# The opening of an adaLN attention and feed-forward block: all input tiles turned before the projections

## The chip, the cores and the metric

The kernel runs on one core of one Trainium2 chip. The metric is the device time of one execution in microseconds. The kernel before was run three times: 855.94, 863.45 and 854.26 us, median 855.94 us. The profile is of one more execution, which took 855.57 us.

## The reference, cut to what matters

```
mod = (silu(c) @ wmod).reshape(1, 6, 1, 512)          # c: (1,512)   wmod: (512, 3072)
sa, ca, ga, sb, cb, gb = mod                           # shift, scale, gate of attention; the same of the FFN
h  = layernorm(x) * (1 + ca) + sa                      # x: (1024, 512)
q  = rmsnorm(h @ wq_a.T) @ wq_b.T                      # latent of 128, then 32 heads of 64 + 64
ckv, k_pe = split(h @ wkv_a.T)                         # latent of 32 and a shared rotary key of 64
k, v = rmsnorm(ckv) @ wkv_b.T                          # 32 heads
attention, causal, rotary on the pe parts, softmax;  x = x + ga * (attention @ wo.T)
h  = layernorm(x) * (1 + cb) + sb
x  = x + gb * ((silu(h @ gate_w.T * gs) * (h @ up_w.T * us)) @ down_w.T * ds)
```

All is kept at the precision of float32: most products are made as three products of a high part and a rest (`xH`, `xL`: the value rounded to the matmul's own format, and what is left of it).

## The kernel before, in words

**The opening** works for eight tiles of 128 rows of x (`st` 0 to 7). For each tile VectorE takes mean and variance, ScalarE the root; `normalise` subtracts and scales; TensorE turns the tile by four transposes (`turn_inputs`, L501); ScalarE applies scale and shift of the modulation while it empties the bank, in four pieces (`modulate`, L766); VectorE makes the high part (`h_high`, L996), GpSimd the rest (`hL`, L1334); TensorE projects the tile on 288 rows of weights with 3 x 4 matmuls (`project_inputs`, L513) and turns the resulting latents (`turn_latents`, L522, L523) after ScalarE and VectorE have normalised them (`roots`, `scale`). `latents_high` and `latents_low` split them into `QNH`, `QNL`, `KH`, `KL`. These steps are written as one pipeline: in turn `st`, tile `st` is turned, tile `st-1` projected, tile `st-3`'s latents turned. h, its high part and its rest have two buffers each.

Before the pipeline TensorE computes the shift and scale columns of the modulation (`mod_columns(0)` and `(1)`, L482): for each of six modulation vectors the weights are 1 MB in `wmod`; as columns they take 16 float32 matmuls, which the trace shows as 32 instructions that load 128x128 weights and move one column. The columns 2 and 3 (scale and shift of the second layer norm) and the two gates as rows (`mod_rows`, L490, 8 instructions with 512 columns for a gate) are computed later in the opening, between other work. The six vectors pass through three buffers in `PR`.

**Groups of heads.** 32 heads are 8 groups (g) of 4. For each group: folded weights (`w`, L535), projection of the queries in two halves of 512 rows (`even`, `odd`, `lat`, L544), the rotary products on VectorE (`even`, `odd`, L1056 to L1064), the sums (`RE`; for group 0 on VectorE, L1069 and L1070, for later ones on GpSimd, L1354 and L1355), high part on ScalarE (L811), rest (`split_low`, GpSimd L1361; group 0 on VectorE, L1088). The SP queue then sends the queries of a half by four DMAs, one for each head, from `TQ` to `Q` (L402). Then 38 `part`s: products of queries and keys (L554, with a causal mask L558) into one of three side banks, whose row maxima VectorE takes (L1096: 27 into NMa, 11 into NMb). `join` (L1102) and `rows` (L564, L1109) make a row of negative maxima, which SP sends to `Q` (L407). Each side item takes the next of three PSUM banks in a fixed order, and TensorE waits for the bank's `free` semaphore before it writes.

**Windows.** Window w (0 to 7) computes scores (L610 to L612), exponentials, values (L625) and sums of group w; between its 36 units a table places side items: the 38 maxima of group w+1, the query work of group w+2, the row sums. `window_table` gives each item a place (a share of the window) and a busy time of VectorE. The first two groups' side items stand in the opening: group 0's queries (`QUERY_PLACES`), then `PROLOGUE`, which holds group 0's maxima, group 1's query work and the two gates as rows. All engines issue in the order written; window 0 begins when SP's row of maxima has landed (`S_.nd`). After the windows come the output projection and the feed-forward part, which the change does not touch.

## Time and profile before

| | |
|---|---|
| three runs | 855.94, 863.45, 854.26 us (median 855.94) |
| profiled execution | 855.57 us; its span, first to last instruction, 853.8 us |
| TensorE matmul busy | 793.7 us, 93% of the span |
| VectorE busy | 551.0 us, 65% |
| ScalarE busy | 272.2 us, 32% |
| GpSimd busy | 146.5 us, 17% |
| DMA | 60.46 MB, mean 71 GB/s |
| opening, to the first score | 135.57 us |
| mean granted TensorE clock | 0.960 |

The opening is everything up to the first score (L610). Matmuls are pipelined and the profile models their ends, so the busy share of TensorE is not its work at its best pace: the start of one instruction against the start of the next tells its pace. A granted clock of 1.00 is 2.4 GHz, one of 0.50 is 1.2 GHz. Start times are counted from the span's start.

### The profile page before, as it was taken

What the parts mean: (1) busy time and instruction counts of PE and PEld (TensorE: products, weight loads), DVE (VectorE), ACT (ScalarE), POOL (GpSimd) and SP (SyncE); (2) the same over time, 40 slices, a digit from 0 to 9 for tenths busy, and PEclk for the clock granted to TensorE, in tenths of its full rate; (3) what the DMA queues carried; (4) which work ended last, traced back from release to release, by engine and by line L of the source; (5) the groups of instructions that cost most, each with busy time, mean ns of one, the idle gap of its engine ahead of it and who ended that gap; (6) DMA issues with size and microseconds to landing.
All of it is one profiled execution on the core that took longest, in us unless ns stands there. A gap on an engine that the chain in (4) does not pass through costs nothing.

```text
span 853.8 us, 10443 instructions
## 1 busy us (share of the span) xinstructions
PE 793.7 (93%) x3968; PEld 530.2 (62%) x3968; DVE 551.0 (65%) x836; ACT 272.2 (32%) x402; POOL 146.5 (17%) x113
## 2 busy tenths in 40 slices
PE   5678897999999999999999999999898899999997
PEld 5667544555555555555555555544587788886886
DVE  3355694896896997988978978867565333222342
ACT  2361003333333333343333333343344232222120
POOL 1320031221221321411302401010134000000111
PEclk9886697999999999999999999999899899999999
DMA  8300724023213303321330335046000032220000
GB/s 345 116 0 1 211 52 111 20 56 89 51 25 89 75 21 69 74 52 38 74 85 5 74 83 214 2 159 212 1 1 0 10 102 74 74 65 1 25 37 38
DMA packets 35904, 60.46 MB, mean 71 GB/s; under 512 B 4144, under 2 KB 16176, under 8 KB 34064
## 3 DMA queue, kind: packets, MB, share of 16 engines
q1 hardware_dynamic: 34656, 57.11, 23.7%
q10 hardware_dynamic: 1200, 2.69, 0.9%
q8 instruction: 33, 0.54, 0.3%
q14 instruction: 15, 0.12, 0.1%
HBM read 32.40 MB, written 2.10 MB: 40 GB/s over the span
## 4 chain that ended last, share of the span: by engine, by line
PE 64%; DVE 20%; issue 9%; POOL 2%; ACT 2%; DMA 2%; SPq 1%; POOLq 0%; DVEq 0%; ACTq 0%
PE PS L710 14%; PE PS L610 6%; PE PS L554 6%; PE PS L625 6%; DVE PR L1184 6%; PE PS L680 5%; PE PS L611 5%; PE PS L612 5%; DVE NMa L1096 4%; DVE NMb L1096 3%; PE PS L544 2%; PE PS L482 2%; PE PS L570 2%; PE PS L513 2%; PE PS L614 2%
## 5 line engine op out<-in xcount | busy, mean ns | idle before, releaser
L836 ACT ACTIVATE PR<-PS 128x1024 f32<-128x1024 f32 (+1 forms) x144 | 133.0, 929 | 255.2 <-PE PS L612 240.4
L1096 DVE TENSOR_REDUCE NMa<-PS 128x1 f32<-128x512 f32 (+3 forms) x216 | 138.7, 662 | 50.0 <-PE PS L558 42.7
L554 PE MATMUL PS<-KH,Q 96*128 96x512 f32 (+3 forms) x384 | 135.5, 414 | 3.9 <-DVE TQ L1081 1.4
L610 PE MATMUL PS<-Q,KH 97*128 97x512 f32 x288 | 131.7, 457 | 2.6 <-DMA Q<-NM 2.6
L710 PE MATMUL PS<-Q 128*128 128x512 f32 (+1 forms) x528 | 123.2, 396 | 5.1 <-DVE Q L1258 4.5
L710 PEld LDWEIGHTS PS<-Q 128*128 128x128 f32 (+1 forms) x528 | 99.2, 188 | 28.2 <-DVE Q L1258 4.7
L1184 DVE TENSOR_TENSOR PR<-PR 128x2048 f32<-128x2048 f32 (+3 forms) x56 | 109.3, 1951 | 10.2 <-ACT PR L836 8.9
L611 PE MATMUL PS<-Q,KL 96*128 96x512 f32 x288 | 114.7, 398 | 0.0
L612 PE MATMUL PS<-Q,KH 96*128 96x512 f32 x288 | 113.9, 396 | 0.0
L554 PEld LDWEIGHTS PS<-KH,Q 96*128 96x128 f32 x384 | 69.8, 197 | 62.3 <-issue 38.0
L610 PEld LDWEIGHTS PS<-Q,KH 97*128 97x128 f32 x288 | 56.0, 195 | 35.3 <-issue 17.1
L625 PE MATMUL PS<-PR,V 128*32 128x512 f32 (+3 forms) x704 | 73.1, 488 | 0.3 <-ACT PR L836 0.3
L612 PEld LDWEIGHTS PS<-Q,KH 96*128 96x128 f32 x288 | 55.1, 191 | 12.9
L611 PEld LDWEIGHTS PS<-Q,KL 96*128 96x128 f32 x288 | 55.4, 192 | 6.6
L1096 DVE TENSOR_REDUCE NMb<-PS 128x1 f32<-128x384 f32 (+3 forms) x88 | 55.3, 629 | 1.0 <-PE PS L558 0.8
L1271 DVE SCALAR_TENSOR_TENSOR wide<-PS,ffn_s,TQ 128x1024 f32<-128x1024 f32 x10 | 12.8, 1285 | 65.9 <-PE PS L710 65.9
L558 PE MATMUL PS<-maskb,identb 128*128 128x128 bf16 (+2 forms) x176 | 46.0, 261 | 0.0
L1367 POOL TENSOR_TENSOR wide<-wide,RD 128x512 f32<-128x512 f32 x16 | 22.7, 1416 | 130.6 <-DVE RD L1123 130.6
L727 PE MATMUL PS<-DH,Q 128*128 128x512 f32 (+1 forms) x176 | 42.8, 391 | 1.4 <-DVE TQ L1271 1.4
L1354 POOL TENSOR_TENSOR RE<-RT 128x512 f32<-128x512 f32 x14 | 18.0, 1286 | 129.3 <-DVE RT L1064 119.4
L1361 POOL TENSOR_TENSOR TQ<-RE,TQ 128x1024 fp32r<-128x1024 f32 x14 | 33.6, 2403 | 36.3 <-ACT TQ L811 36.3
L1412 POOL TENSOR_TENSOR OT<-TQ,Y 128x512 f32<-128x512 f32 x8 | 10.3, 1290 | 168.3 <-DVE Y L1291 168.3
(157 smaller groups left out, 1002.1 us busy)
## 6 DMA issues: line engine op xcount, KB each, us to landing
Q<-TQ SPq DMA_DIRECT2D x64, 384.0 KB, 5.3
PR<-in_wmod SPq DMA_DIRECT2D x6, 1024.0 KB, 7.0
RT<-in_wo SPq DMA_DIRECT2D x4, 1024.0 KB, 5.1
TQ<-in_wo SPq DMA_DIRECT2D x4, 1024.0 KB, 4.9
WI<-in_gate_w SPq DMA_DIRECT2D x10, 256.0 KB, 3.1
WI<-in_up_w SPq DMA_DIRECT2D x10, 256.0 KB, 3.3
DI<-in_down_w SPq DMA_DIRECT2D x10, 256.0 KB, 3.6
TQ<-in_x ACTq DMA_DIRECT2D x2, 1024.0 KB, 10.3
```

What stands on the lines that cost most here:

```text
L554: ins = pe.matmul(bank[:, i * w:(i + 1) * w], M.Q[0:KR, g % 2, 0, qt // 4, h0 + i, qs], M.KH[0:KR, lo:lo + w], start=(i == 0), stop=(i == ...
L558: ins = pe.matmul(corner, M.identb[:], M.maskb[:].unsqueeze(1).broadcast_to([P, n, P]), start=False, stop=True)
L610: pe.matmul(dst, M.KH[0:KR + 1, ks], M.Q[0:KR + 1, w % 2, 0, qb, :, qs], start=True, stop=False)
L611: pe.matmul(dst, M.KL[0:KR, ks], M.Q[0:KR, w % 2, 0, qb, :, qs], start=False, stop=False)
L612: ins = pe.matmul(dst, M.KH[0:KR, ks], M.Q[0:KR, w % 2, 1, qb, :, qs], start=False, stop=not diagonal)
L625: ins = pe.matmul(PS[h * L:(h + 1) * L, 4, QB - wd:QB], M.V[:, kt, :], M.slot(s)[:, h, 0:wd], start=(kt == 0), stop=(kt == blocks_of(qb) - 1))
L680: ins = pe.matmul(PS[:, b, :], a[:, b, g, :], w[:, g, :], start=(n == 0 and g == 0), stop=(n == 2 and g == G - 1))
L710: ins = pe.matmul(PS[0:m, 4 * b + 2 * w + hf, :], a[:, b, w, k, 0:m], h[:, k, hf * 512:(hf + 1) * 512], start=(n == 0 and k == 0), stop=(n ...
L727: ins = pe.matmul(PS[:, b, :], a[b][0:k, ch, :], w[0:k, ch, :], start=(n == 0 and ch == 0), stop=(n == 2 and rest == 1))
L836: act.activation(tiles, banks, ACT.Exp).then_inc(S_.p, 1)
L1096: dve.tensor_reduce(dst, PS[:, bank_of(turn), 0:n * w].rearrange("p (h k) -> p h k", k=w), axis=AX.X, op=ALU.max, negate=True).then_inc(S_ ...
L1184: dve.tensor_tensor(sums, sums, M.slot(s)[:, :, 0:wd], ALU.add).then_inc(S_.ad, 1)
```

## The change

It rewrites the opening and touches the first two windows.

- x comes in eight transfers of one tile on the SP queue (before: two halves on the ScalarE queue), into its own buffer; the first four tiles, modulation vector 1 (shift), the other four, vector 0 (scale), then the 288 rows of projection weights, the rotary table for keys, the small vectors and the folded weights' inputs of groups 0 and 1.
- All eight tiles are normalised (now ScalarE, in place, with `shift` = -mean x rstd), turned, and split into high part (ScalarE, from PSUM) and rest (VectorE, from PSUM) ahead of any projection; each tile keeps its own buffers. TensorE computes vector 1 after tile 1, vector 0 after tile 5, and `shift_projected` after tile 6.
- The modulation of h is gone: the scale goes into the projection weights (four ScalarE copies with a scale, four VectorE operations for the rest), the shift into a row of 288 values, computed by four float32 matmuls and added to each tile by two matmuls of one row.
- Then projections: tile `st` is projected, the latents of `st-2` turned. The last two steps of a key (`V`, rotary sum) go from VectorE to GpSimd (`keys`). The two small roots of a tile become one. The latents use one bank (4) where they used two.
- Group 0's folded weights come after tile 1; its first half of queries (512 rows) right after tile 6's projection, the second half after the last tile. The first half's rotary sums and rest go to GpSimd.
- Group 1 (`HANDED`): ScalarE copies the even and odd queries out of PSUM, GpSimd makes the four products and two sums; ScalarE also makes the latent's high part.
- The gates as rows and columns 2 move into window 0 (places 0.55, 0.65, 0.72), columns 3 into window 1 (0.10). Their weights are loaded in window 0, into a part of `wide`. SP waits there until TensorE has computed gate 0 and only then issues the last load, the first half of group 2's queries and the next row of maxima.

```diff
...
+HANDED = (1,)
...
+        self.scb = self.wide[:, 1, 0:D].rearrange("p (k n) -> p k n", k=KD)
+        late_mod = [self.wide[:, 2 + 2 * n:4 + 2 * n, :].rearrange("p c (k d) -> p (c k) d", d=D) for n in range(3)]
+        self.wmod = [self.PR[:, 0], self.PR[:, 1], late_mod[2], late_mod[0], late_mod[0], late_mod[1]]
...
+def group_places(g, places):
+
+    return [(place, (name[0], g) + name[1:], 0.0 if name[0] in ("even", "odd") and g in HANDED else busy)
...
+    if w == 0:
+        places += [(0.55, ("modrow", 0, 0), 0.7), (0.65, ("modrow", 0, 1), 0.7), (0.72, ("mod", 0, 2), 0.2)]
+    if w == 1:
+        places.append((0.1, ("mod", w, 3), 0.2))
...
+FIRST_FOLDS = [("w", 0, i) for i in range(3)]
+FIRST_QUERIES = [[(kind, 0, hf) for kind in ("even", "odd", "lat", "split")] for hf in range(2)]
+
+FIRST_MAXIMA = [key for _, key, _ in sorted(group_places(0, maxima_places(0.04, 0.84)) + group_places(1, QUERY_PLACES),
+                                            key=lambda x: x[0])]
...
     sp.dma_start(M.cT[:], t["c"]).then_inc(S_.c, 16)
+    for st in range(NS):
+        sp.dma_start(M.x[:, st, :], xt[:, st, :]).then_inc(S_.x[st], 16)
+        if st == 3:
+            load_mod(1)
     load_mod(0)
-    load_mod(1)
+    sp.dma_start(M.WA[:], t["wa"]).then_inc(S_.wa, 16)
+    sp.dma_start(M.rope_k[:], t["rope_k"]).then_inc(S_.rope, 16)
     for dst, name in ((M.lnq, "lnq"), (M.lnkv, "lnkv"), (M.ffn_s, "ffn_s")):
         sp.dma_start(dst[:], t[name]).then_inc(S_.small, 16)
-    sp.dma_start(M.rope_k[:], t["rope_k"]).then_inc(S_.rope, 16)
-    for n in (2, 3, 4):
-        load_mod(n)
+    load_weights(0)
     sp.dma_start(M.cos[:], t["cos"]).then_inc(S_.tables, 16)
     sp.dma_start(M.sin[:], t["sin"]).then_inc(S_.tables, 16)
-    load_weights(0)
+    load_weights(1)
     sp.wait_ge(S_.one, 1)
     send_queries(0, 0)
     send_queries(0, 1)
...
             send_queries(w + 1, 1)
+        if w == 0:
+            for n in (4, 5, 2):
+                load_mod(n)
+            sp.wait_ge(S_.side, TURN[("modrow", 0, 0)] + 1)
...
+    def mod_columns(n, dst):
         pe.wait_ge(S_.wm[n], 16)
-        if n >= 2:
-            pe.wait_ge(S_.mc, n - 1)
+        for d in range(KD):
+            for k in range(KD):
+                ins = pe.matmul(dst[:, d:d + 1], M.wmod[n][:, k, d * P:(d + 1) * P], M.silu_c[:, k:k + 1],
+                                start=(k == 0), stop=(k == KD - 1))
+        return ins
+
+    def mod_rows(n, dst):
+        pe.wait_ge(S_.wm[4 + n], 16)
+        pe.wait_ge(S_.scb, 1)
         for k in range(KD):
-            ins = pe.matmul(dst[:, d:d + 1], M.PR[:, n % 3, k, d * P:(d + 1) * P], M.silu_c[:, k:k + 1],
-                            start=(k == 0), stop=(k == KD - 1))
-        if d == KD - 1:
-            ins.then_inc(S_.m, 1)
...
+    def shift_projected():
+        pe.wait_ge(S_.wa, 16)
+        pe.wait_ge(S_.mc, 1)
+        for k in range(KD):
+            ins = pe.matmul(PS[0:1, 5, 0:ROWS], M.mod_col[:, 1, k:k + 1], M.WA[:, k, :], start=(k == 0), stop=(k == KD - 1))
+        ins.then_inc(S_.m, 1)
...
     def turn_inputs(st):
         b = st % 2
         pe.wait_ge(S_.xn, st + 1)
         if st >= 2:
-            pe.wait_ge(S_.full, st - 1)
+            pe.wait_ge(S_.lo, st - 1)
         for d in range(KD):
-            ins = pe.transpose(PS[:, b, d * P:(d + 1) * P], M.xn[:, b, d * P:(d + 1) * P], M.ident[:])
+            ins = pe.transpose(PS[:, b, d * P:(d + 1) * P], M.x[:, st, d * P:(d + 1) * P], M.ident[:])
         ins.then_inc(S_.tr, 1)
 
     def project_inputs(st):
         b = st % 2
-        pe.wait_ge(S_.lo, st + 1)
-        if st == 0:
-            pe.wait_ge(S_.wal, 1)
+        pe.wait_ge(S_.hi, st + 1)
+        pe.wait_ge(S_.wah, 1)
         if st >= 2:
             pe.wait_ge(S_.cr, st - 1)
-        for n, (h, w) in enumerate(((M.hH, M.WAH), (M.hL, M.WAH), (M.hH, M.WAL))):
+        pe.wait_ge(S_.lo, st + 1)
+        for n, (h, w) in enumerate(((M.hH[:, st], M.WAH), (M.hL[st], M.WAH), (M.hH[:, st], M.WAL))):
+            if n == 2:
+                pe.wait_ge(S_.wal, 1)
             for k in range(KD):
-                ins = pe.matmul(PS[:, 2 + b, 0:ROWS], h[:, b, k, :], w[:, k, :], start=(n == 0 and k == 0),
-                                stop=(n == 2 and k == KD - 1))
+                pe.matmul(PS[:, 2 + b, 0:ROWS], h[:, k, :], w[:, k, :], start=(n == 0 and k == 0), stop=False)
+        pe.wait_ge(S_.one, 2)
+        pe.wait_ge(S_.bias, 2)
+        for hl in range(2):
+            ins = pe.matmul(PS[:, 2 + b, 0:ROWS], M.oner[:], M.bias[:, hl, :], start=False, stop=hl == 1)
         ins.then_inc(S_.pj, 1)
...
+        half = PS[:, 4, :]
         pe.wait_ge(S_.kr, st + 1)
-        if st >= 2:
-            pe.wait_ge(S_.ql, st - 1)
-        pe.transpose(PS[:, 4 + b, 0:P], M.qn[:, b, :], M.ident[:])
-        pe.transpose(PS[0:KR, 4 + b, P:2 * P], M.key[:, b, :], M.ident[:]).then_inc(S_.t2, 1)
+        if st >= 1:
+            pe.wait_ge(S_.ql, st)
...
-    for n in range(2):
-        for d in range(KD):
-            mod_columns(n, d, PS[:, 6 + n, 0:KD])
-    for st in range(NS + 3):
+    for st in range(NS):
+        turn_inputs(st)
+        if st == 1:
+            mod_columns(1, PS[:, 7, 0:KD]).then_inc(S_.m, 1)
+        if st == 5:
+            mod_columns(0, PS[:, 6, 0:KD]).then_inc(S_.m, 1)
+        if st == 6:
+            shift_projected()
+    for st in range(NS + 2):
         if st < NS:
-            turn_inputs(st)
-        if 0 <= st - 1 < NS:
-            project_inputs(st - 1)
-        if 0 <= st - 3 < NS:
-            turn_latents(st - 3)
-
+            project_inputs(st)
+        if 0 <= st - 2 < NS:
+            turn_latents(st - 2)
+        if st == 1:
+            for key in FIRST_FOLDS:
+                side(key)
+        if st == NS - 2:
...
+    for key in FIRST_QUERIES[1] + FIRST_MAXIMA:
+        side(key)
...
+        act.wait_ge(S_.wa, 16)
+        act.wait_ge(S_.mc, 2)
+        for k in range(KD):
+            ins = act.activation(M.WAH[:, k, :], M.WA[:, k, :], ACT.Copy, scale=M.mod_col[:, 0, k:k + 1])
+        ins.then_inc(S_.wah, 1)
+
+    def normalise_input(st):
+        act.wait_ge(S_.rs, 2 * st + 2)
+        act.activation(M.x[:, st, :], M.x[:, st, :], ACT.Identity, scale=M.rstd[:, st:st + 1],
+                       bias=M.shift[:, st:st + 1]).then_inc(S_.xn, 1)
+
+    def h_high(st):
         act.wait_ge(S_.tr, st + 1)
-        if st >= 2:
-            act.wait_ge(S_.lo, st - 1)
-        for d in range(KD):
-            ins = act.activation(M.full[:, b, d, :], PS[:, b, d * P:(d + 1) * P], ACT.Identity,
-                                 scale=M.mod_col[:, 0, d:d + 1], bias=M.mod_col[:, 1, d:d + 1])
-        ins.then_inc(S_.full, 1)
+        act.activation(M.hH[:, st].rearrange("p k n -> p (k n)"), PS[:, st % 2, :], ACT.Copy).then_inc(S_.hi, 1)
...
+    def queries_copied(kind, g, hf):
+        turn = TURN[(kind, g, hf)]
+        act.wait_ge(S_.side, turn + 1)
+        act.wait_ge(S_.re, 2 * (2 * g + hf))
+        act.activation(M.RT[:, ("even", "odd").index(kind), :], PS[:, bank_of(turn), :], ACT.Copy).then_inc(
+            S_.free[turn % 3], 1)
+
+    def latent_high(g, hf):
+        turn = TURN[("lat", g, hf)]
+        cols = slice(hf * 512, hf * 512 + 512)
+        for h in range(HG):
+            act.wait_ge(S_.q[hf][h], 16 * g)
+        act.wait_ge(S_.side, turn + 1)
+        act.activation(M.TQ[:, 2, 0, cols], PS[:, bank_of(turn), :], ACT.Copy).then_inc(S_.lh, 1)
 
...
+    def inverse_root(st):
+        dve.wait_ge(S_.sq, st + 1)
+        dve.reciprocal(M.rstd[:, st:st + 1], M.rstd[:, st:st + 1]).then_inc(S_.rs, 1)
+        dve.wait_ge(S_.rs, 2 * st + 1)
+        dve.tensor_scalar(M.shift[:, st:st + 1], M.mv[:, st, 0:1], M.rstd[:, st:st + 1], -1.0, ALU.mult,
+                          ALU.mult).then_inc(S_.rs, 1)
+
+    def mod_first(n):
+        dve.wait_ge(S_.m, 2 - n)
+        dve.tensor_scalar(M.mod_col[:, n, :], PS[:, 6 + n, 0:KD], 1.0 if n == 0 else 0.0, None, ALU.add).then_inc(S_.mc, 1)
+
+    def weights_rest():
+        dve.wait_ge(S_.wah, 1)
+        for k in range(KD):
+            ins = dve.scalar_tensor_tensor(out=M.WAL[:, k, :], in0=M.WA[:, k, :], scalar=M.mod_col[:, 0, k:k + 1],
+                                           in1=M.WAH[:, k, :].bitcast(F32), op0=ALU.mult, op1=ALU.subtract)
+        ins.then_inc(S_.wal, 1)
+
+    def shift_split():
+        dve.wait_ge(S_.m, 3)
+        dve.tensor_copy(M.bias[:, 0, :], PS[0:1, 5, 0:ROWS]).then_inc(S_.bias, 1)
+        dve.wait_ge(S_.bias, 1)
+        dve.tensor_tensor(M.bias[:, 1, :], PS[0:1, 5, 0:ROWS], M.bias[:, 0, :].bitcast(F32), ALU.subtract).then_inc(S_.bias, 1)
+
+
+    def h_low(st):
+        dve.wait_ge(S_.hi, st + 1)
+        dve.tensor_tensor(M.hL[st].rearrange("p k n -> p (k n)"), PS[:, st % 2, :],
+                          M.hH[:, st].rearrange("p k n -> p (k n)").bitcast(F32), ALU.subtract).then_inc(S_.lo, 1)
...
         dve.tensor_tensor(sums, sums, M.slot(s)[:, :, 0:wd], ALU.add).then_inc(S_.ad, 1)
...
-            if name[2] == KD - 1:
-                gate_copied(name[1])
-        else:
-            side((name[0], 1, name[1]) if name[-1] == "next" else (name[0], 0) + name[1:])
+    moments(0)
+    moments(1)
+    for st in range(NS):
+        inverse_root(st)
+        if st + 2 < NS:
+            moments(st + 2)
+        if st > 0:
+            h_low(st - 1)
+        if st == 3:
+            mod_first(1)
+    mod_first(0)
+    h_low(NS - 1)
+    weights_rest()
+    shift_split()
+    dve.wait_ge(S_.small, 48)
+    dve.tensor_scalar(M.lnq[:], M.lnq[:], softmax_scale(), None, ALU.mult).then_inc(S_.lnq, 1)
+    dve.wait_ge(S_.rope, 16)
+    for st in range(NS + 2):
+        if st < NS:
+            scale(st)
+        if 0 <= st - 2 < NS:
+            latents_low(st - 2)
+        if st == 1:
+            for key in FIRST_FOLDS:
+                side(key)
+        if st == NS - 2:
+            dve.wait_ge(S_.tables, 32)
+            for key in FIRST_QUERIES[0][:3]:
+                side(key)
+        if st == NS - 1:
+            side(FIRST_QUERIES[0][3])
+    for k in range(KD):
+        ins = dve.tensor_scalar(M.scb[:, k, :].rearrange("p (n l) -> p n l", l=L),
+                                M.ones[:].unsqueeze(1).broadcast_to([P, P // L, L]), M.silu_c[:, k:k + 1], None, ALU.mult)
+    ins.then_inc(S_.scb, 1)
+    for key in FIRST_QUERIES[1] + FIRST_MAXIMA:
+        side(key)
     for w in range(G):
...
+        b = st % 2
+        rot = M.rot[:, b].rearrange("p r (c n) -> p r c n", c=2)
+        pool.wait_ge(S_.cr, st + 1)
+        pool.tensor_copy(M.V[:, st, :], M.key_parts(b)[:, 2])
+        pool.tensor_tensor(M.key_parts(b)[:, 0:2], rot[:, 0], rot[:, 1], ALU.add).then_inc(S_.kr, 1)
 
...
+    def rotate_even(g, hf):
+        cols = slice(hf * 512, hf * 512 + 512)
+        half = 2 * (g - 1) + hf
+        pool.wait_ge(S_.free[TURN[("even", g, hf)] % 3], freed(("even", g, hf)))
+        pool.tensor_tensor(M.RT[:, 3, :], M.RT[:, 0, :], M.sin[:, cols], ALU.mult).then_inc(S_.rp, 1)
+        pool.wait_ge(S_.rp, 4 * half + 1)
+        pool.tensor_tensor(M.RT[:, 0, :], M.RT[:, 0, :], M.cos[:, cols], ALU.mult).then_inc(S_.rp, 1)
+
+    def rotate_odd(g, hf):
+        cols = slice(hf * 512, hf * 512 + 512)
+        half = 2 * (g - 1) + hf
+        pool.wait_ge(S_.free[TURN[("odd", g, hf)] % 3], freed(("odd", g, hf)))
+        pool.tensor_tensor(M.RT[:, 2, :], M.RT[:, 1, :], M.cos[:, cols], ALU.mult).then_inc(S_.rp, 1)
+        pool.wait_ge(S_.rp, 4 * half + 3)
+        pool.tensor_tensor(M.RT[:, 1, :], M.RT[:, 1, :], M.sin[:, cols], ALU.mult).then_inc(S_.rp, 1)
+        pool.wait_ge(S_.rp, 4 * half + 4)
+        pool.wait_ge(S_.tl, 2 * g + hf)
+        pool.tensor_tensor(M.RE[:, 0, :], M.RT[:, 0, :], M.RT[:, 1, :], ALU.subtract).then_inc(S_.re, 1)
+        pool.tensor_tensor(M.RE[:, 1, :], M.RT[:, 2, :], M.RT[:, 3, :], ALU.add).then_inc(S_.re, 1)
...
```

## Rows read from the trace of the kernel before

**Rows 1.** Timeline, SP queue: maxima sent (start, length, queue line, transfer)

```profile
133.32 0.56 SPq L407 DMA_DIRECT2D Q<-NM  x1
193.21 0.56 SPq L407 DMA_DIRECT2D Q<-NM  x1
254.28 0.56 SPq L407 DMA_DIRECT2D Q<-NM  x1
...
498.53 0.56 SPq L407 DMA_DIRECT2D Q<-NM  x1
549.04 0.56 SPq L407 DMA_DIRECT2D Q<-NM  x1
```

**Rows 2.** Busy time by stretch: length, PE, PEld, DVE, ACT, POOL, clock, DMA, GB/s

```profile
257.00:318.00 61.00, 59.56 (x329) 34.42 (x325) 51.44 (x73) 22.28 (x25) 13.40 (x9) 1.00 0.25 58
```

**Rows 3.** Chain that ended last, in order of time, the opening (start, length, what)

```profile
28.48 3.25 PE PS L513 x12
31.72 0.87 PE PS L501 x4
...
60.81 1.92 PE PS L513 x12
...
65.28 0.18 DVE V L1012
...
89.33 1.24 DVE TQ L1088
...
98.87 2.98 DMA WK<-in_wk
...
120.77 0.91 PE PS L490 x2
...
131.65 0.82 DVE NMa L1102
...
133.32 2.12 DMA Q<-NM
...
135.57 0.76 PE PS L610
```

**Rows 4.** Groups by line, 28.2 to 66.5 us (count, busy us, mean ns, idle before)

```profile
L1334 POOL TENSOR_TENSOR hL<-full,hH 128x512 fp32r<-128x512 f32 x8 | 10.9, 1357 | 27.1 <-DVE hH L996 27.1
...
L513 PE MATMUL PS<-WAH,hH 128*128 128x288 f32 x32 | 9.5, 443 | 11.4 <-POOL hL L1334 11.4
```

**Rows 5.** Timeline of the start (start, length, engine, instruction, idle before)

```profile
7.90 0.69 DVE L956 BATCH_NORM_STATS2 stats<-TQ 128x6 f32<-128x512 f32 x1 [7.90 <-DMA TQ<-in_x]
...
9.17 13.78 PE L482 MATMUL PS<-silu_c,PR 128*128 128x1 f32 x64 [9.17 <-DMA PR<-in_wmod]
```

**Rows 6.** Timeline, group 0's queries sent and its maxima begun

```profile
83.85 5.46 PE L482 MATMUL PS<-silu_c,PR 128*128 128x1 f32 x32
...
84.34 11.89 SPq L402 DMA_DIRECT2D Q<-TQ  x8
...
89.18 0.67 PE L554 MATMUL PS<-KH,Q 96*128 96x384 f32 x1
```

**Rows 7.** Groups by line, 89 to 132 us

```profile
L1096 DVE TENSOR_REDUCE NMa<-PS 128x1 f32<-128x512 f32 (+3 forms) x27 | 17.0, 662 | 4.5 <-PE PS L554 2.2 <-PE PS L558 2.2
...
L1361 POOL TENSOR_TENSOR TQ<-RE,TQ 128x1024 fp32r<-128x1024 f32 x2 | 4.7, 2356 | 2.6 <-ACT TQ L811 2.6
...
L1096 DVE TENSOR_REDUCE NMb<-PS 128x1 f32<-128x384 f32 (+3 forms) x11 | 7.0, 632 | 0.0
...
L1354 POOL TENSOR_TENSOR RE<-RT 128x512 f32<-128x512 f32 x2 | 2.6, 1286 | 14.6 <-issue 10.0 <-DVE RT L1064 4.6
...
L1056 DVE TENSOR_TENSOR RT<-PS,cos 128x512 f32<-128x512 f32 x2 | 1.4, 684 | 0.6 <-PE PS L544 0.6
```

**Rows 8.** Stretches, TensorE alone: length, busy (count), granted clock, DMA, GB/s

```profile
84.50:85.50 1.00, 1.00 (x10) 0.92 0.00 0
85.50:95.50 10.00, 10.00 (x36) 0.50 0.93 223
95.50:96.50 1.00, 1.00 (x7) 0.96 0.96 256
```

More of the change, by code:

```diff
@@ L167, in __init__ @@
         self.stats = take("stats", [P, NS, 6])
+        self.shift = take("shift", [P, NS])
         self.mv = take("mv", [P, NS, 2])
         self.rstd = take("rstd", [P, NS])
+        queries = self.at
         self.Q = take("Q", [P, 2, 2, NQB, HG, QB], F32R)
@@ L815, in side @@
             weights_high(key[1])
+        elif key[0] in ("even", "odd") and key[1] in HANDED:
+            queries_copied(key[0], key[1], key[2])
+        elif key[0] == "lat" and key[1] in HANDED:
+            latent_high(key[1], key[2])
         elif key[0] == "split":
@@ L1064, in odd @@
         dve.tensor_tensor(M.RT[:, 2, :], PS[:, bank_of(turn), :], M.cos[:, cols], ALU.mult).then_inc(S_.free[turn % 3], 1)
-        if g == 0:
-            dve.wait_ge(S_.free[turn % 3], freed(("odd", g, hf)))
-            if hf == 1:
-                dve.wait_ge(S_.tl, 1)
+        if (g, hf) == (0, 1):
+            for kind in ("even", "odd"):
+                dve.wait_ge(S_.free[TURN[(kind, g, hf)] % 3], freed((kind, g, hf)))
+            dve.wait_ge(S_.tl, 1)
             dve.tensor_tensor(M.RE[:, 0, :], M.RT[:, 0, :], M.RT[:, 1, :], ALU.subtract).then_inc(S_.re, 1)
@@ L1150, in side @@
             weights_folded(g, key[2])
-        elif kind == "even":
+        elif kind == "even" and g not in HANDED:
             even(g, key[2])
-        elif kind == "odd":
+        elif kind == "odd" and g not in HANDED:
             odd(g, key[2])
@@ L1156, in side @@
             latent(g, key[2])
-        elif kind == "split" and g == 0:
+        elif kind == "split" and (g, key[2]) == (0, 1):
             split_low_first(key[2])
@@ L1328, in pool_program @@
     pool.wait_ge(S_.one, 1)
[L1329 to L1334 removed]
+    pool.memset(M.oner[:].bitcast(F32), 1.0).then_inc(S_.one, 1)
+    pool.wait_ge(S_.one, 2)
     pool.memset(M.identb[:], 0.0).then_inc(S_.mask, 1)
@@ L1372, in side @@
             weights_low(g)
-        elif kind == "odd" and g > 0:
+        elif kind == "even" and g in HANDED:
+            rotate_even(g, key[2])
+        elif kind == "odd" and g in HANDED:
+            rotate_odd(g, key[2])
+        elif kind == "odd" and (g, key[2]) != (0, 1):
             rotate(g, key[2])
-        elif kind == "split" and g > 0:
+        elif kind == "split" and (g, key[2]) != (0, 1):
             split_low(g, key[2])
```

313 lines of the change are left out of this document (129 added, 184 removed).

## The prediction, made before the change was run

> **What bounds the kernel now.** I read first the SP queue's timeline for the lengths of the windows [rows 1]. Maxima of group 0 leave at 133.32 us, those of group 1 at 193.21, of group 2 at 254.28, so a window takes 59.9 to 61.1 us. Window 6, which has no query work, takes 549.04 - 498.53 = 50.5. Work put into or taken out of a window shows in its length: there is no slack that swallows it. The busy time of a full window says why [rows 2]: TensorE 59.6 of 61 us, at full clock, VectorE 51.4. Everything ahead of the first score at 135.57 us is a different regime, and the chain of waits there [rows 3] passes through every engine in turn: eight tiles until 65.5, folded weights and half of group 0's queries, the second half done at 90.6 (L1088), then maxima until 131.65, then a fixed tail of 135.57 - 131.65 = 3.9 us (join, row, transfer). In the tiles TensorE waits 11.4 us in all for GpSimd's rest of h, and GpSimd for VectorE's high part before it [rows 4]: a round trip per tile and pair of buffers. So the opening is latency, and the windows are TensorE's throughput. The change trades one for the other.
>
> **The new opening, first part: to the first projection.** The first megabyte of x and of modulation weights landed at 7.90 and 9.17 us [rows 5]; x now comes first in 0.25 MB pieces, so tile 0 is there at about 4 and vector 1 at about 8.6 (an estimate from those two). Columns cost 13.78/64 = 0.215 us each [rows 5], 6.9 us for a vector. TensorE: tiles 0 and 1 turned before 8.9; vector 1 to 15.8; tiles 2 to 5. A turn is 0.87 us [rows 3], but tile st needs the rest of st-2 out of its bank, and VectorE has 0.69 of statistics [rows 5] and, taken as equal, 0.7 of subtraction, with some 0.5 of small ones and waits, so about 1.9 a tile: tile 5 is turned at 22.6. Vector 0 to 29.5, tile 6 to 30.4. Then the shift row: 4 products in float32 of 288 columns. A gate's product, two instructions of 512 columns, takes 0.91 at full clock [rows 3]; by columns that is 0.51, at half clock 1.0, so 4.0 us and 34.4. Tile 7 to 35.3; then ScalarE's high part and four scaled copies of the weights. No row has these; GpSimd, the slowest engine for such work, takes 1.36 for 512 columns [rows 4], so the 512 and 1152 columns together are 4.4 at most and, at VectorE's 0.68 [rows 7], 2.2 at least. I take 2.7, near the faster end since only GpSimd was waited for in the old pipeline: **38**. Before, the first projection began at 28.48: 9.5 us later now.
>
> **Second part: projections.** Twelve matmuls took 3.25 us at the start and 1.92 later [rows 3]; fourteen take 3.8 or 2.2. By the earlier pace the first is at 42; afterwards TensorE is hardly idle, as nothing is waited for but the tile two back: from the last projection's end at 62.73 to its latents read at 65.46 [rows 3] are 2.7 us, less than two tiles. With the latents' transposes I take 2.2 to 2.4 a tile; group 0's folds add 1.3. Tile 6 ends at 56, the first half's nine query matmuls at 58.6, tile 7 at 60.5. VectorE's four rotary products and two latent operations (6 x 0.68 [rows 7] less overlap: 3.7) reach 61; GpSimd makes two sums of 1.29 and a rest of 2.36 [rows 7], ScalarE about 1 between: first half ready at **67**. VectorE turns then to tile 7, and `keys(7)` stands behind those sums on GpSimd: 63. Tiles 6 and 7 finish at 66; half 1 takes 7.3 more: before, the halves were ready 90.57 - 84.34 = 6.2 apart [rows 3, 6], with the matmuls (1.0) hidden: **73.3**. Before: 90.6. Gain so far 17.
>
> **Third part: maxima.** The queries landed 89.18 - 84.34 = 4.8 us or less after issue [rows 6]; eight transfers take 11.89 to issue, 1.5 each. So maxima begin at 71.8, the second half's heads come at 78 to 82.5. VectorE has 38 maxima, 24.0 us busy [rows 7], 22 with overlap, plus group 1's folds (1.0) and two latent rests (1.3). Gone: eight rotary products (0.6 apart, 4.8), two latent high parts, two gates (1.3) and the wait of 3 us for WK, which stood on SP behind eight sends and is loaded early now. After the first half (78.8): 15.7 + 1.3 = 17 to 95.8. To this I add **2.5**: half 0 of group 1 takes GpSimd 6 x 1.29 + 2.36 = 10.1, from about 79.3, ScalarE 1 between, to 90.7; the even queries of half 1 are projected at about 85, but ScalarE stands at the split of half 0 until 88.2, two of three side banks stay full, and TensorE waits with all maxima behind it. SP: group 1's first four sends stand ahead of the row of maxima, 90.7 to 95.3, done in time. So 98.5, and the tail of 3.9 makes **102.5**. The opening gives 135.57 - 102.5 = **33 us**.
>
> On GpSimd the rows show 1286 ns against VectorE's 684 for the same 128x512 [rows 7], and VectorE is what this stretch runs out of. The Trainium skill (GPSIMD Engine Reference, Engine selection) says to keep two-input elementwise work on VectorE, as GpSimd is about twice as slow. The trace agrees (1.9 times); followed, the rule would give VectorE 4.8 us back and take the 2.5 away, an opening longer by 2.3.
>
> **Paid back in the windows.** Each gate's 8 instructions: 4 x 0.91 = 3.6 us at full clock [rows 3]; two are 7.2. Columns 2 and 3: 32 instructions took 5.46 us [rows 6], 1.6 of it at full clock; then, with the engine never idle and doing nothing but columns, the granted clock fell to 0.50 and stayed there until 95.5 [rows 8]. In a window the matmuls after them start at half clock too; from dense work's start at 135.57 and at 89.18 it took 4 and 6 us to rise. Four us at half pace lose 2, so 7.5 a vector, 15 for two. VectorE's copies (two of 0.7) lie beside TensorE's. Gates and columns together **22**; the two ends are 7.2 + 2 x 3.7 = 15 (0.115 each, clock never falls) less a few us of cover, some 11, and 7.2 + 2 x 8.7 = 24.5 (half clock as long as in that row). I take 21. The four megabytes loaded in window 0 are free: its DMA share is 0.25 in such a window [rows 2]. SP waits for gate 0 at place 0.55 and issues group 2's half some 3 to 5 us later than before; window 1 needs it, and it has 25 us: nothing.
>
> The Trainium skill (TensorE: Matmul & The Clock Gate, What's actually happening) has the gate follow how busy the array was; read plainly, back-to-back columns are busy, and the two vectors would cost 7.4 in place of 15. The row above contradicts it: the clock fell in their midst.
>
> **Sum.** 33 - 21 = 12 off the profiled execution's 855.6: 843.6. It stands 0.4 below the median of the three runs, so 844 of a median; I say **843.5**.
>
> **The rivals.**
> A, the forecast: 836 to 850. Chance 0.48.
> B, cheap windows: the clock doesn't fall, or rises at once, cost about 11, and the opening gives 33: 833 (826 to 836). For it: the clock held for the first 1.5 us of the columns [rows 8], and where the gate's turn falls in a vector is open. Against: window 6's length, which shows no slack. 0.20.
> C, a weaker opening: group 1's chain on GpSimd (2 x 11 us from 79.3 on, so 102 at the end) holds the side banks for both halves, odd queries of half 1 copied at 96 and a third of the maxima, 8 us, behind them: first score at 108 to 112; gain 33 - 9 = 24, less 21: 852.5 (850 to 857). 0.22.
> D, slower: TensorE's clock. Its share was 0.5 through a stretch of ten us in which it was never idle [rows 8]. If it is at half from 38 us on, projections take 8 x 3.8 + transposes, 11 more, and the maxima become TensorE's (48 products, 22 masks, 18 query matmuls at half pace, some 32 us against VectorE's 25): 6 more. Opening 16, windows 24.5: 864. It decides from a mean granted clock of about 0.6 between 40 and 95 us. Against: the projections reached 1.92 per twelve even in the old, gappy pipeline. 0.10.
>
> **How the numbers follow.** This kernel's runs tell about 1%, 8.6 us, from no change. Faster by more: A below 847.3 (0.41) and B (0.20), 0.61. Slower by more: half of D, 0.05. Same: the rest, 0.34. Range: B's lower quarter (0.06) and D with C's end (0.12) are left out: 829 to 857.
>
> **What would show it.** First score at 98 to 107 us, first projection at 36 to 40, queries ready near 67 and 73. Columns of 32 instructions in windows 0 and 1 followed by clock 0.50; window 0 at 74 to 78 us, window 1 at 66 to 70, windows 2 to 7 and the rest as now. The forecast is wrong if a window takes the columns for under 4 us, if the projection pace is 3.8, or if TensorE stands over 5 us behind ScalarE's copies of group 1.

## The result, and the profile after

The changed kernel takes 863.11 us (median of 12 runs, 853.84 to 866.63); the kernel before, run beside it, 854.98 (851.55 to 863.45). The ratio of the means is 1.0083 [1.0048, 1.0117], the 95% interval in brackets: slower by 0.8%, where 843.5 and a gain of 12 were forecast. The profiled execution took 862.31, its span is 860.3. Of the 12 runs, eleven lie at 861.6 or above with a mean granted clock of 0.946 to 0.950; one, at 853.84, had 0.959. So runs of one kernel can differ by some 9 us, and the faster has the higher clock.

The maxima sent, on SP's timeline, are to be read beside [rows 1]:

```profile
110.30 0.56 SPq L417 DMA_DIRECT2D Q<-NM  x1
191.37 0.56 SPq L417 DMA_DIRECT2D Q<-NM  x1
261.76 0.56 SPq L417 DMA_DIRECT2D Q<-NM  x1
322.83 0.55 SPq L417 DMA_DIRECT2D Q<-NM  x1
...
556.53 0.57 SPq L417 DMA_DIRECT2D Q<-NM  x1
```

Differences give the ledger. The opening ends 133.32 - 110.30 = 23.0 us earlier. Window 0 takes 81.1 instead of 59.9 (+21.2), window 1 70.4 instead of 61.1 (+9.3). Windows 2 on are as before; what follows 556.53 is 1.0 shorter. Together -23.0 + 21.2 + 9.3 - 1.0 = +6.5, the difference of the two spans (860.3 - 853.8).

The chain that ended last, in the opening (start, length, what), is to be read beside [rows 3]:

```profile
73.64 0.70 DVE TQ L1117
74.36 0.88 DVE TQ L1124
75.51 0.56 DVE NMa L1132
...
85.33 0.61 ACT RT L829
86.00 1.30 POOL RT L1437
...
92.58 1.24 POOL RE L1451
...
93.93 0.04 ACT TQ L846
...
94.89 0.59 ACT RT L829
...
108.48 0.66 DVE NMb L1132
109.27 0.19 DVE NMa L1138
...
110.30 2.19 DMA Q<-NM
```

VectorE begins its first maximum at 75.5, straight behind the second half's low part (L1117, L1124). The four rotary products and two sums of group 1's first half hold GpSimd from 86.0 to 93.8; ScalarE's split (L846) waits for them, and its copy of the next block (L829) is queued behind the split, at 94.89. By lines, 75.5 to 109.1 us, VectorE's maxima (count, busy, mean ns, idle before):

```profile
L1132 DVE TENSOR_REDUCE NMa<-PS 128x1 f32<-128x512 f32 (+3 forms) x27 | 17.3, 665 | 2.7 <-PE PS L588 1.5 <-PE PS L584 1.1
L1132 DVE TENSOR_REDUCE NMb<-PS 128x1 f32<-128x384 f32 (+3 forms) x11 | 7.0, 638 | 3.4 <-PE PS L588 3.4
L1117 DVE TENSOR_TENSOR TQ<-PS,TQ 128x512 fp32r<-128x512 f32 x2 | 1.4, 692 | 2.2 <-ACT TQ L838 2.2
```

Its idle time in this stretch is 2.7 + 3.4 + 2.2 = 8.3 us, where VectorE's own work was meant to be the limit. TensorE's moved items, from its timeline:

```profile
163.69 3.60 PE L506 MATMUL PS<-wide 128*128 128x512 f32 x8
...
173.11 3.60 PE L506 MATMUL PS<-wide 128*128 128x512 f32 x8
...
178.31 4.80 PE L498 MATMUL PS<-silu_c,wide 128*128 128x1 f32 x32
...
200.03 6.13 PE L498 MATMUL PS<-silu_c,wide 128*128 128x1 f32 x32
```

And stretches, TensorE alone (length, busy and count, granted clock, DMA, GB/s), read as [rows 8]:

```profile
92.00:112.50 20.50, 15.73 (x40) 0.50 0.36 82
112.50:132.50 20.00, 19.97 (x60) 0.50 0.80 248
132.50:134.00 1.50, 1.50 (x10) 0.92 0.00 0
...
180.50:187.50 7.00, 7.00 (x29) 0.51 0.01 2
...
201.00:214.50 13.50, 13.50 (x51) 0.50 0.13 29
```

Each burst of columns is followed by half clock, as forecast, but for 7.0 and 13.5 us and not for 4. New is the second row: the first score is at 112.53, from there TensorE is busy for 19.97 of 20.0 us, and all of it goes at half clock. Before, the clock rose 4.4 us after the first score.

### The profile page after: what moved, and what is told of

Same layout as the page of the kernel before. It is cut to its first block, busy times and chain, and to the rows that moved or that the text cites. A ratio compares the mean times of both kernels' runs of the same rounds, so it can differ in the third digit from the quotient of the medians.

```text
span 860.3 us, 10490 instructions
## 1 busy us (share of the span) xinstructions
PE 807.8 (94%) x3992; PEld 534.5 (62%) x3992; DVE 542.2 (63%) x819; ACT 275.4 (32%) x393; POOL 152.2 (18%) x132
## 4 chain that ended last, share of the span: by engine, by line
PE 64%; DVE 16%; issue 8%; POOL 2%; ACT 1%; DMA 1%; POOLq 0%; DVEq 0%; ACTq 0%
PE PS L740 14%; PE PS L584 7%; PE PS L644 7%; PE PS L659 6%; PE PS L645 6%; PE PS L646 6%; PE PS L710 5%; DVE PR L1235 5%; DVE NMa L1132 3%; DVE NMb L1132 3%; PE PS L574 2%; PE PS L600 2%; PE PS L648 2%; PE PS L588 2%; PE PS L498 1%
## 5 line engine op out<-in xcount | busy, mean ns | idle before, releaser
L584 PE MATMUL PS<-KH,Q 96*128 96x512 f32 (+3 forms) x384 | 140.3, 431 | 4.8 <-DVE TQ L1117 3.7
L644 PE MATMUL PS<-Q,KH 97*128 97x512 f32 x288 | 134.1, 466 | 2.8 <-DMA Q<-NM 2.8
L740 PEld LDWEIGHTS PS<-Q 128*128 128x128 f32 (+1 forms) x528 | 99.2, 188 | 28.2 <-DVE Q L1331 4.7
L645 PE MATMUL PS<-Q,KL 96*128 96x512 f32 x288 | 116.7, 405 | 0.0
L646 PE MATMUL PS<-Q,KH 96*128 96x512 f32 x288 | 115.9, 403 | 0.0
L584 PEld LDWEIGHTS PS<-KH,Q 96*128 96x128 f32 x384 | 74.5, 210 | 61.7 <-issue 38.7
L588 PE MATMUL PS<-maskb,identb 128*128 128x128 bf16 (+2 forms) x176 | 48.5, 276 | 0.0
L757 PE MATMUL PS<-DH,Q 128*128 128x512 f32 (+1 forms) x176 | 42.8, 391 | 1.4 <-DVE TQ L1344 1.4
L1457 POOL TENSOR_TENSOR TQ<-RE,TQ 128x1024 fp32r<-128x1024 f32 x15 | 36.1, 2407 | 37.2 <-ACT TQ L846 37.2
L757 PEld LDWEIGHTS PS<-DH,Q 128*128 128x128 f32 (+1 forms) x176 | 33.0, 188 | 8.8 <-DVE TQ L1344 1.9
```

Of the source, the lines that this page charges most:

```text
L584: ins = pe.matmul(bank[:, i * w:(i + 1) * w], M.Q[0:KR, g % 2, 0, qt // 4, h0 + i, qs], M.KH[0:KR, lo:lo + w], start=(i == 0), stop=(i == ...
L588: ins = pe.matmul(corner, M.identb[:], M.maskb[:].unsqueeze(1).broadcast_to([P, n, P]), start=False, stop=True)
L644: pe.matmul(dst, M.KH[0:KR + 1, ks], M.Q[0:KR + 1, w % 2, 0, qb, :, qs], start=True, stop=False)
L645: pe.matmul(dst, M.KL[0:KR, ks], M.Q[0:KR, w % 2, 0, qb, :, qs], start=False, stop=False)
L646: ins = pe.matmul(dst, M.KH[0:KR, ks], M.Q[0:KR, w % 2, 1, qb, :, qs], start=False, stop=not diagonal)
L740: ins = pe.matmul(PS[0:m, 4 * b + 2 * w + hf, :], a[:, b, w, k, 0:m], h[:, k, hf * 512:(hf + 1) * 512], start=(n == 0 and k == 0), stop=(n ...
```

## The experiments

All in one table: the first send of maxima, the lengths of windows 0 and 1 from SP's timeline, how long the clock stayed at half behind the first score, and the median time. All but the last column come from one profiled execution of each kernel; where that one lies far from the median, the text says so. The kernel before had medians of 855 to 859 beside these runs; ratios of means to it stand in the text.

| kernel | send | w 0 | w 1 | half | us |
|---|---|---|---|---|---|
| before | 133.3 | 59.9 | 61.1 | 4.4 | 855.0 |
| after | 110.3 | 81.1 | 70.4 | 20.0 | 863.1 |
| w_none | 111.2 | 67.0 | 61.1 | 20.0 | 838.8 |
| w_gates | 111.5 | 66.4 | 60.4 | 3.8 | 839.7 |
| lateload | 110.3 | 81.1 | 70.4 | 20.0 | 863.9 |
| nohand | 114.6 | 82.3 | 68.8 | 23.2 | 867.0 |
| allopen | 121.0 | 60.0 | 61.1 | 4.2 | 845.0 |
| cols_open | 117.4 | 66.7 | 60.4 | 4.3 | 848.4 |
| fill | 113.6 | 71.8 | 68.8 | 0 | 852.7 |
| fill_end | 110.8 | 70.4 | 70.4 | 0.4 | 854.5 |
| spread | 110.1 | 75.6 | 66.5 | 20.0 | 858.0 |
| gates_open | 114.5 | 74.2 | 69.3 | 23.2 | 859.8 |
| gates_spread | 113.6 | 70.1 | 67.5 | 23.1 | 853.1 |
| before_nogates | 130.9 | 68.3 | 61.1 | 22.9 | 861.4 |
| gates_open_fill | 114.8 | 63.4 | 68.1 | 0 | 846.1 |
| allopen_fill | 118.1 | 58.0 | 61.1 | 0 | 838.4 |
| allopen_again | 118.4 | 68.8 | 61.1 | 23.7 | 846.6 |
| before_fill | 133.6 | 58.3 | 61.1 | 0.7 | 853.0 |

**What the moved work costs.** Two kernels leave work out of the windows, with constants in place of its results (the edits below are cut to what matters; w_gates keeps the gates of the first line and leaves out its third item).

```diff
# w_none: loads, gates and columns left out; w_gates: only the columns and their loads
-        places += [(0.55, ("modrow", 0, 0), 0.7), (0.65, ("modrow", 0, 1), 0.7), (0.72, ("mod", 0, 2), 0.2)]
-        places.append((0.1, ("mod", w, 3), 0.2))
```

> Leaves out the two gates and the columns 2 and 3 of the modulation (their products and loads; constants stand in their place); the opening is that of the changed kernel. It prices all that went into windows 0 and 1, which grew by 21.2 and 9.3 us. Theory 1 (the moved work and the clock it pulls down is the whole of it): window 0 back to 60 to 61 us, window 1 to 61, time 862 - 30 = 832. Theory 2 (the opening leaves the clock at half and window 0 stays at half for 20 us whatever is in it): window 0 at 68, window 1 at 61, time 840.

> Leaves out the columns 2 and 3 alone; the gates and their two loads stay in window 0. Theory 1: the two gates cost 6.9 us and their loads the long half clock, 8; window 0 at 75, window 1 at 61, time 847. If the long half clock comes from the opening, the same 847 or so, as it is there anyway; if it comes from the third load alone, 839. Rival: columns cost as little as 3.7 us each and leave no trace: 855.

Ratios 0.9796 [0.9738, 0.9854] and 0.9825 [0.9782, 0.9867]: 24 us hang on this work. But with all of it gone window 0 still took 67.0 us, with the clock at half until 133.5. With the gates back the profiled run's clock rose at 117.5, and window 0 was no longer: the shorter stay paid for the gates. So the slow start is a cost of its own. It also varies: of w_none's four runs one took 832.8 with a clock of 0.967, three took 838 to 844 with 0.955 to 0.959; of w_gates' four, three took 839.7 with 0.967 and one 845.7 with 0.957.

**Do the four megabytes loaded into window 0 cause it?**

```diff
         if w == 0:
+            sp.wait_ge(S_.side, TURN[("part", 1, 12)] + 1)
             for n in (4, 5, 2):
```

> The changed kernel with the three loads of window 0 (3 MB) issued only when TensorE has reached the thirteenth maximum of group 1, about a quarter into the window. Theory 1a (the loads that run from 117 to 130 us hold the clock at half, which rises 3 us after they end): clock at full 4 to 6 us after the first score as in the kernel before, window 0 shorter by 8, time 854; perhaps some half clock later where the loads now run. Theory 1b (the loads have nothing to do with it): clock at half until 132 us as now, time 862.

863.94, ratio 1.0094 [1.0058, 1.013], sends at the same times, and the clock again at half until 132.5. No: when these loads run makes no difference to the slow start.

**Is it right to give group 1's rotary products and sums to GpSimd?**

```diff
-HANDED = (1,)
+HANDED = ()
```

> Group 1's queries go back to VectorE (HANDED empty), all else as in the changed kernel. Theory 1 (side banks are held by ScalarE's copies, which wait for GpSimd's chain: VectorE sat idle some 9 of 34 us): first score 3 to 5 us earlier, at 108, in spite of 4.8 us more on VectorE; time 858. Rival (VectorE's own work is the bound of the maxima): first score 4 to 5 us later, at 117; time 867.

867.01, ratio 1.0068 [1.0017, 1.0118], in which the two slowest of the ten runs are left out; the first send is 4.3 us later. The runs form two groups, as those of the changed kernel do: four at 856.1 to 856.8 (clock 0.956) and six at 866.6 to 870.7 (0.938 to 0.941), against one at 853.8 and eleven at 861.6 to 866.6. So group beside group it is some 3 to 5 us slower. My first theory fell; the rival's numbers held. The Trainium skill (GPSIMD Engine Reference, Engine selection) would keep two-input elementwise work on VectorE; the prediction put that at 2.3 us more in the opening, and the profiles show 4.3 more: followed here, the rule doesn't pay. The size need not be VectorE's work alone. In nohand TensorE's clock stood at half from 75 us on, in the changed kernel only from 92.0, and VectorE still waited 6 us, nearly all of it for TensorE; what the move costs at the same clock was not measured. The stretch in nohand, TensorE alone:

```profile
75.00:113.00 38.00, 33.90 (x92) 0.50 0.41 93
```

**The moved work put back into the opening**, all of it, the columns alone, the gates alone (cut; the weights' loads move ahead of window 0 with it):

```diff
+    for d in range(KD): mod_piece(3, d)      # column 2 among the last projections
+    ... + [(0.1 + 0.35 * n + 0.08 * k, ("gaterow", n, k), 0.0) ...]   # gates among the maxima
-        places += [... ("modrow", 0, 0) ..., ("modrow", 0, 1) ..., ("mod", 0, 2) ...]
```

> The rest of the change stays; the modulation columns 2 and 3 (32 one-column matmuls) go back into the opening, and the two gates' rows (8 of 512 columns) too, among the maxima of the first half-windows. Theory (the place is the price): the opening pays about what window 0 and 1 paid in busy time or less, first maxima sent 112 to 118 us instead of 110.3; window 0 falls from 81.1 to 60 to 67 us, window 1 from 70.4 to 61.1; span about 860.3 + 5 - 17 - 9.3 = 839, time 836 to 843. Rival 1 (the gates and columns cost the same wherever they stand): first maxima sent at 110.3 + 30 = 140, time 860 to 863. Rival 2 (TensorE's low granted clock at the start of window 0 is part of the faster opening whatever fills it): window 0 stays at 67 us as with both left out, time about 843; if the gates' rows ahead of the first score bring the clock back, window 0 takes 60 and the time is 836.

> Only the modulation columns 2 and 3 go back into the opening, the gates' rows stay in window 0. Theory: window 1 falls from 70.4 to 61.1 us and window 0 from 81.1 to about 73 to 75 (gates 7 and the slow start 6 to 7 remain above 60); the opening is 1 to 3 us longer; time 863.1 - 9.3 - 7 + 2 = 849 (845 to 853). Rival (the gates are the costly part of window 0, not the columns): window 0 stays at 78 or more and the time at 854 or above.

> Only the two gates' rows go back into the opening, by pieces among the maxima; the columns 2 and 3 stay in one burst each in windows 0 and 1. Theory (the gates' dense rows both leave window 0 and bring TensorE's clock to full earlier): first maxima sent at 112 to 115 instead of 110.3, clock full by 125 us, window 0 65 to 67, window 1 70.4 as before, time 848 to 852. Rival (the clock stays at half to 132 us with the gates in the opening too): window 0 72 or more, time 857 or above.

Ratios 0.985 [0.9759, 0.9941], 0.9868 [0.9805, 0.9931], 1.0053 [1.0022, 1.0084]. The place is the price: in the opening gates and columns cost 8 to 11 us of first send (allopen_again below, allopen), in the windows 30 with the longer slow start. cols_open came out as forecast by two misses that cancel: its opening grew by 7.1 us and not by 1 to 3, its window 0 took 66.7 and not 73 to 75, since the clock rose 4.3 us behind the first score. For the gates alone my theory fell. Dense rows among the maxima did not bring the clock back; it was at half for 23 us behind the first score.

**Burst or spread?** The columns in four pieces each, a few score units apart.

```diff
-(0.72, ("mod", 0, 2), 0.2)
+*((0.72 + 0.06 * d, ("mod", 0, 2, d), 0.2) for d in range(KD))
-places.append((0.1, ("mod", w, 3), 0.2))
+places += [(0.1 + 0.1 * d, ("mod", 1, 3, d), 0.2) for d in range(KD)]
```

> The changed kernel with the modulation columns 2 and 3 of windows 0 and 1 cut into four pieces each (one column of the result per piece), a few score units apart; work and place are the same otherwise. Theory (the dear part of the moved columns is TensorE's clock at half behind a burst of 32 short matmuls, not the 4.6 us of the burst): no fall of the clock to half in windows 0 and 1 behind the columns; window 1 falls from 70.4 to 65 to 67 us, window 0 from 81.1 to 76 to 78, time 854 to 857. Rival (the columns cost their busy time and the side banks' turns wherever they stand): windows 70 and 81, time 862 to 866.

> The gates' rows in the opening and the columns 2 and 3 in four pieces each in windows 0 and 1. If both theories hold: first maxima sent at 112 to 115, window 0 62 to 65, window 1 65 to 67, time 842 to 846, which is below the kernel before. Rival: the pieces cost as the bursts, time 848 to 852.

857.98, ratio 0.9978 [0.993, 1.0026], and 853.09, 0.9974 [0.9939, 1.0009]; the first 1 us above its forecast, the second 7, with its clock again at half for 23 us at the start; 5 and 7 us below the same kernel with bursts. In spread's profile window 0 is 5.5 us shorter and window 1 3.9, but that execution took 852.26, 5.7 below the median of its ten; why seven of them took 856.5 to 858.6 no profile shows. The stretch of window 1 that stood at half clock in the changed kernel is now, in the run spread (3.4 us at half are left elsewhere in it):

```profile
200.00:214.50 14.50, 14.50 (x94) 1.00 0.00 1
```

**Work added to fill TensorE's gaps.** Matmuls of 512 columns, their result unused. The edit of fill adds more than its expectation says: its trace shows 32, one behind each of the last 26 maxima's scores and six behind the row. fill_end has the six alone.

```diff
+        if key[0] == "part" and key[2] >= 12: filler(1)     # fill only
+        if key[0] == "rows": filler(6)                      # fill and fill_end
```

> The changed kernel with extra matmuls of 512 columns whose result is not used: one after each of the last four score blocks' maxima matmuls of the opening and six behind the first group's rows, just ahead of the first score. They add work only. Theory (the long stay of TensorE's clock at half, 92.0 to 132.5 us, comes from what TensorE did in the gaps of 92 to 112 us, which the gates' rows used to fill): the granted clock is full by about 118 us, window 0 is 5 to 8 us shorter than 81.1, the time 855 to 859 in spite of the added work. Rival (the long stay is independent of what stands in the gaps): the clock is again at half to 130 us or longer, window 0 81 us, and the added work shows at its price of 0.2 to 0.45 us each: 863 to 866.

> As the run before it with only the six extra matmuls behind the first group's rows. Theory of the gaps: less than the ten of the run before it: clock full by 118 to 125 us, time 857 to 862. Rival: as the changed kernel or up to 2 us above, 863 to 865.

852.72 and 854.46: with more work the changed kernel is 9 to 10 us faster (ratios to before 0.9931 [0.9896, 0.9965] and 0.9954 [0.9905, 1.0004]), 2 to 3 below the lower ends forecast. The clock is full at the first score in fill and 0.4 us behind it in fill_end. The time that window 0 lost at its start, 9 to 11 us of 81.1, was TensorE's clock.

**The same question to the kernel before.** The gates' rows are left out, constants in their place.

```diff
         if name[0] == "modrow":
-            mod_rows(name[1], name[2])
+            pass
```

> The kernel before with the two gates' rows left out (not computed, constants in their place). It asks in the kernel before whether these rows of 512 columns kept TensorE's clock up ahead of window 0. Theory: the opening is 3 to 7 us shorter, but the clock is at half for 12 to 20 us behind the first score instead of 7 (133.3 to 140), window 0 is 63 to 67 us instead of 59.9, and the time is 851 to 856, about that of the kernel before. Rival (the clock's return has nothing to do with them): window 0 stays at 60 and the time is 848 to 851.

861.4, ratio 1.0031 [0.9981, 1.0082]: the two gates' eight products of 512 columns less, and not faster. Three of its ten runs took 851.5 to 855.2, seven 861.3 to 862.9; the kernel before, beside it, has 23 runs at 851.5 to 856.2 and eight at 860.2 to 865.5. Its stretches, TensorE alone:

```profile
122.00:128.50 6.50, 3.75 (x15) 1.00 0.66 158
128.50:133.00 4.50, 0.37 (x1) 0.53 0.06 18
133.00:156.00 23.00, 22.87 (x69) 0.50 0.34 79
156.00:157.50 1.50, 1.50 (x8) 0.98 0.00 0
```

The clock is full until TensorE falls idle for the last maxima and their way through DMA; it drops there and stays down for 23 us of unbroken work.

**Where the stay begins.** gates_open shows the two gaps on TensorE's timeline (idle in brackets):

```profile
113.80 0.37 PE L605 MATMUL PS<-ident,NMa 128*32 128x128 f32 x1 [1.49 <-DVE NMa L1152]
116.84 0.77 PE L657 MATMUL PS<-Q,KH 97*128 97x512 f32 x1 [2.67 <-DMA Q<-NM]
```

Three of the last four experiments fill just these: three matmuls behind the last maximum's scores, six behind the row; allopen_again has none.

```diff
+        if (key[0] == "part" and key[2] == len(PARTS) - 1) or key[0] == "rows":
+            for _ in range(6 if key[0] == "rows" else 3):
+                pe.matmul(PS[:, 4, :], M.QNH[:, 0:P], M.QNH[:, 0:512], start=True, stop=True)
```

> As the kernel with only the gates' rows in the opening, with extra matmuls of 512 columns whose result is not used in the last two idle stretches of TensorE ahead of the first score: three behind the last maxima's scores, six behind the rows. Theory (the long stay at half starts from the idle just ahead of the first score): the clock is full from 120 us at the latest instead of 140.0, window 0 falls from 74.2 to 64 to 68 us, the time from 859.8 to 849 to 853. Rival (what stands in these gaps doesn't matter, the stay is a matter of the state the clock came in): half to 135 us or later, 858 to 861.

> The kernel with gates and columns in the opening, with the same nine extra matmuls. Theory: its stay at half (121.0 to 127.5 us) goes, the first score is up to 1 us later, window 0 falls from 60.0 to 57 to 58 us; time 839 to 843, and a narrower spread from run to run. Rival: as without them, 842 to 847.

> The kernel with gates and columns in the opening once more, as the measure for the run before it and for the ratio to the kernel before: 842 to 847, ratio 0.98 to 0.99.

> The kernel before with the same nine extra matmuls in its last two idle stretches ahead of the first score (1.8 us ahead of the rows, 2.6 us behind them). Theory: the stay at half of 129.5 to 140.0 us goes, window 0 falls from 59.9 to 57 to 58 us at up to 1 us more in the opening: 851 to 853, and the runs near 863 us, which the kernel before has in one of four, become rare. Rival: as the kernel before, 855 with the same spread.

gates_open_fill takes 846.07 (845.18 to 846.6), ratio 0.9847 [0.9786, 0.9909], 13.7 us below the kernel without the fillers. The same stretch in gates_open, then in gates_open_fill:

```profile
113.00:117.00 4.00, 0.53 (x2) 0.50 0.15 39
117.00:140.00 23.00, 23.00 (x70) 0.50 0.58 167
```

```profile
113.00:117.00 4.00, 2.11 (x9) 1.00 0.09 20
117.00:140.00 23.00, 22.70 (x127) 1.00 0.58 171
```

70 matmuls became 127 in the same 23 us. The gap ahead of the first score had only shrunk, from 2.67 to 1.29 us.

allopen_fill takes 838.35 (834.75 to 839.21), ratio **0.9751** [0.9686, 0.9815]: it beats both kernels. Its first windows, SP's timeline:

```profile
118.07 0.56 SPq L415 DMA_DIRECT2D Q<-NM  x1
176.06 0.56 SPq L415 DMA_DIRECT2D Q<-NM  x1
237.18 0.56 SPq L415 DMA_DIRECT2D Q<-NM  x1
```

allopen_again (846.55, ratio 0.985 [0.9777, 0.9924]) is the same kernel without fillers, and the same as allopen; its profiled execution, 849.89, is the slowest of its four. Their two profiles, first allopen, then allopen_again:

```profile
121.00:123.50 2.50, 0.23 (x1) 0.50 0.22 61
123.50:127.50 4.00, 4.00 (x11) 0.50 0.80 175
127.50:144.50 17.00, 17.00 (x98) 0.99 0.29 63
```

```profile
117.00:120.50 3.50, 0.37 (x1) 0.53 0.08 16
120.50:144.50 24.00, 23.74 (x71) 0.50 0.33 77
```

One program, once 4 and once 24 us at half clock; window 0 took 60.0 and 68.8. The whole execution differed by 6.4 us, since the second one's opening was 2.5 us shorter. So without fillers the stay can be short or long in one and the same program. before_fill (853.03, 0.9978 [0.9935, 1.0022]) shortens window 0 by 1.6 us, to 58.3 where 57 to 58 was expected, but its time is not told from the kernel before's, and two of ten runs were still above 860.

## Why the prediction was wrong

- **First projection at 38:** 37.83 (the rows lacked ScalarE's scaled copies, but the kernel before's trace had one: 1.15 us for 1152 columns at L757). **First half's queries at 67:** 67.21. **TensorE begins the maxima at 71.8:** 71.34. Right.
- **Second half at 73.3:** its low part starts at 74.4 and ends at 75.2. Off by 2; TensorE's nine query matmuls for it took 3.95 us (67.39 to 71.34) where the first half's took 2.19 (56.34 to 58.53).
- **Failed: the third part, maxima to 98.5 and first score at 102.5.** The first score came at 112.53, so the opening gave 23.0, not 33. It failed in two places. I let VectorE begin maxima at 71.8 beside the second half's products; both are VectorE's, in written order, and the products come first: first maximum at 75.5, 4 us. And I allowed 2.5 us for the chain of banks, ScalarE and GpSimd; VectorE idled 8.3. GpSimd's chain was forecast to begin at 79.3 and began at 86.0; ScalarE's copy was expected free of the split by 88.2 and stood behind it until 94.9. This was rival C's mechanism, its 108 to 112 the measured time but for half a microsecond. Together 4 + 6 = 10. Not all of the 8.3 need be that chain: 4.6 of it fell behind 92.0, where TensorE's clock was at half and its query matmuls started 0.43 us apart, not 0.23. No run parts the two.
- **Paid back, 21 to 22: right as a sum, its terms less so.** From allopen_fill (58.0) to gates_open_fill (63.4) column 2 costs 5.4, forecast 7.5; from there to fill (71.8) the gates cost 8.4, forecast 7.2; column 3 costs 9.3 in window 1, forecast 7.5. Sum 23.1, against 22 by the working; that the misses cancel is luck. The 4 us at half behind a burst had the wrong size: column 3 cost 9.3, 7.7 and 7.0 us with 13.5, 10.2 and 6.8 us at half in its window (after, fill, gates_open_fill).
- **Failed by omission: the clock at the start of window 0.** I carried [rows 8] only to places behind columns, and in rival D to the projections and maxima. At the first score I took the old 4 us for given. After: 20 us at half. allopen_again against allopen_fill prices it, 68.8 - 58.0 = 10.8 for 23.7 us; after's window 0 is 9.3 above fill's, before's 4.4 us cost 59.9 - 58.0 = 1.9. Missed: 9.3 - 1.9 = 7.4.
- **Sum:** the forecast was -12; 10 of the opening, 7.4 of the clock and 2.1 more of gates and columns than the 21 taken make +7.5, less 1.0 behind the windows: +6.5, as measured. Window lengths of different kernels went into these terms, so that each may be off by 1 or 2 us; the total agrees because it was taken apart, not because each term was measured by itself. The upper end, 857, had room for C but not for C with a slow start.
- **Rival D** gave 864 and was right in the number alone, which is luck. It asked for a clock of about 0.6 between 40 and 95 us; the row shows 0.82, and the stretch at half came later, in the last 17 us of the maxima:

```profile
40.00:95.00 55.00, 44.97 (x210) 0.82 0.28 64
95.00:112.00 17.00, 12.73 (x34) 0.50 0.42 94
```

- **Free loads, SP's wait for gate 0:** no sign against them (lateload, and windows 2 on unchanged).

What stays open: why the clock, once down at the first score, rises after 4 us in some executions and after 20 to 24 in others. Ruled out are the loads (lateload), the gates' rows among the maxima as a remedy (gates_open), and a difference of program (allopen and allopen_again). The gap alone doesn't decide it either: before, w_gates, allopen and cols_open had the same 2.6 to 2.7 us ahead of the first score and rose after 4. Nor did every long stay begin there: in after, w_none, lateload and spread the clock had been at half since 92.0, 20 us ahead of the first score. Shown is that work in the gaps (in fill, among the maxima as well) takes the stay away: all 18 runs of fill, gates_open_fill and allopen_fill have a mean granted clock of 0.968 or more; of fill_end and of before_fill two runs in ten fell back (0.948, and 0.952 to 0.954).
